# Feed-forward stages: the second half of an item's row maxima is transposed into the mixed bank instead of the tokens bank

## The reference

```python
x = _layernorm(x + self_attention(x))               # stage 1, causal
x = _layernorm(x + cross_attention(x, ctx, mask))   # stage 2, 64 keys
for l in range(2):                                  # inside _L0_ffn_ref
    x = x + _attn(_ln(x, ln1_w[l], ln1_b[l]), ...)  # stages 3 and 4, causal
    h = _ln(x, ln2_w[l], ln2_b[l])
    x = x + (_token_moe if l == 0 else _seq_moe)(h, ...)
x = _layernorm(...)
```

## Time and profile before

| | |
|---|---|
| median of 3 runs | 1364.99 us (1358.8, 1364.99, 1370.07) |
| profiled execution, device time | 1360.42 us |
| its span, first to last instruction | 1358.6 us |
| mean granted TensorE clock | 0.948 |
| PE busy | 1226.1 us (90%), 9884 instructions |
| DVE busy | 931.0 us (69%) |
| ACT busy | 806.2 us (59%) |
| POOL busy | 685.0 us (50%) |
| chain that ended last, by engine | PE 63%, DVE 14%, POOL 10%, issue 6%, ACT 4% |
| `L638` PE into tokens, count | 384, 54.1 us busy, 21.4 us idle before |
| `L830` ACT copy of a half | 577 ns each |

### The profile page before, as it was taken

One profiled execution on the slowest core, in us unless ns is written; L12 is line 12 of the kernel. 1 busy time (PEld: TensorE's weight loads), 2 busy tenths in 40 slices (PEclk: granted clock), 3 DMA queues, 4 the chain that ended last, 5 costly groups with the idle time before them and its releaser, 6 DMA issues.

```text
span 1358.6 us, 30590 instructions
## 1 busy us (share of the span) xinstructions
PE 1226.1 (90%) x9884; PEld 996.7 (73%) x9884; DVE 931.0 (69%) x2791; ACT 806.2 (59%) x1629; POOL 685.0 (50%) x1233
## 2 busy tenths in 40 slices
PE   2999999998888789999999899979999999989997
PEld 1777777776666467777777799878777777768886
DVE  5789998987667778888995221123888888645553
ACT  3577776664565356666666565544666666664443
POOL 4355555563222136777778310220567666445554
PEclk9899999986787779999998999998999999999999
DMA  4687777524555444545541787777565555346764
GB/s 110 177 226 236 215 229 201 130 69 128 151 159 145 123 118 126 133 132 135 132 125 46 200 239 226 230 223 210 155 147 148 145 147 150 101 117 187 203 195 118
DMA packets 212707, 216.94 MB, mean 160 GB/s; under 512 B 46403, under 2 KB 163395, under 8 KB 212548
## 3 DMA queue, kind: packets, MB, share of 16 engines
q1 hardware_dynamic: 197712, 199.52, 54.4%
q0 software_dynamic: 4096, 8.40, 2.2%
q10 hardware_dynamic: 10740, 7.06, 1.7%
HBM read 126.90 MB, written 85.46 MB: 156 GB/s over the span
## 4 chain that ended last, share of the span: by engine, by line
PE 63%; DVE 14%; POOL 10%; issue 6%; ACT 4%; SPq 1%; DMA 1%; ACTq 1%; DVEq 0%; POOLq 0%
PE weights L1556 6%; PE scores L609 5%; PE weights L663 4%; PE values L699 4%; PE scores L1799 3%; PE weights L1815 3%; PE weights L668 3%; POOL out_room L1251 3%; POOL probs L1160 3%; PE values L706 3%; PE scores L618 3%; PE scores L1540 3%; DVE negmax L1004 3%; PE tokens L562 2%; PE mixed L718 2%
## 5 line engine op out<-in xcount | busy, mean ns | idle before, releaser
L1160 POOL TENSOR_SCALAR_AFFINE_SELECT probs<-probs 128x256 f32<-128x256 f32 (+1 forms) x576 | 279.0, 490 | 233.8 <-ACT probs L849 230.2
L849 ACT ACTIVATE probs<-weights 128x512 f32<-128x512 f32 x448 | 264.6, 597 | 118.0 <-PE weights L663 84.3
L1004 DVE TENSOR_REDUCE negmax<-scores 128x4 f32<-128x512 f32 x384 | 260.8, 684 | 78.1 <-PE scores L609 74.7
L609 PE MATMUL scores<-keys,queries 128*128 128x512 f32 (+1 forms) x384 | 185.1, 485 | 3.5 <-DVE negmax L1004 1.0
L849 ACT ACTIVATE probs<-weights,keybias 128x512 f32<-128x512 f32 x192 | 131.3, 688 | 65.5 <-PE weights L663 48.4
L663 PE MATMUL weights<-queries,keys 104*128 104x256 f32 x768 | 159.1, 290 | 0.9 <-issue 0.6
L663 PEld LDWEIGHTS weights<-queries,keys 104*128 104x128 f32 x768 | 139.9, 194 | 22.3 <-issue 3.6
L1008 DVE TENSOR_REDUCE negmax<-scores 128x2 f32<-128x512 f32 (+1 forms) x192 | 130.7, 684 | 29.9 <-PE scores L615 20.2
L668 PEld LDWEIGHTS weights<-queries,keys 104*128 104x128 f32 x768 | 114.4, 195 | 10.3 <-ACT probs L849 0.4
L668 PE MATMUL weights<-queries,keys 104*128 104x128 f32 x768 | 109.9, 267 | 0.3 <-ACT probs L849 0.3
L699 PE MATMUL values<-probs,v 128*32 128x256 f32 x1536 | 105.4, 393 | 2.3 <-POOL probs L1160 2.3
(11 more groups left out here) (275 smaller groups left out, 2791.2 us busy)
## 6 DMA issues: line engine op xcount, KB each, us to landing
windows<-parts SPq DMA_DIRECT2D x192, 192.0 KB
queries<-windows SPq DMA_DIRECT2D x64, 384.0 KB
hidden_room<-in_m_w SPq DMA_DIRECT2D x78, 256.0 KB, 2.9
out_room<-in_m_w SPq DMA_DIRECT2D x78, 256.0 KB, 3.1
keys<-windows SPq DMA_DIRECT2D x192, 96.0 KB
routed_rows<-zeros SPq DMA_DIRECT2D x64, 256.0 KB, 3.6
windows<-parts SPq DMA_DIRECT2D x64, 120.0 KB
expert_rows<-probs ACTq DMA_DIRECT2D x46, 128.0 KB, 3.4
```

The source lines that it names most:

```text
L609: i = pe.matmul(bank[:], queries[0:rows, s, t * P:(t + 1) * P], keys[0:rows, s::S4, half * P:(half + 1) * P], start=True, stop=True)
L849: act.activation(probs[:, n % RING], weight_banks[n % 2][:], ACT.Exp, scale=SCALE, **bias).then_inc(exp_done.sem, 1)
L1004: i = dve.tensor_reduce(most[:, part, s, :], bank[:].rearrange("p (a k) -> p a k", k=P), AX.X, ALU.max, negate=True)
L1160: pool.affine_select(out=block, in_=block, compare_op=ALU.is_ge, fill=0.0, base=0, pattern=[[0, heads], [1, P]], channel_multiplier=-1).th ...
```

## The change

The bank is now a function of the item and of the half. For ffn items the first half stays in `tokens` and the second goes to `mixed`; self and ctx items are as before. The matmuls and copies are the same in number and shape, and no slot or rank changes. What moves are the waits of `take` and `until`: the second half asks for `mixed`, and the next user of `mixed` asks for the second half's copy.

```diff
-        def maxima_bank(g):
-            return mixed_bank if units[g].kind == "ctx" else tokens_bank
+        def maxima_bank(g, half):
+
+            return mixed_bank if units[g].kind == "ctx" or units[g].kind == "ffn" and half else tokens_bank
 
         def pe_maxima(pe, g):
 
-            bank = maxima_bank(g)
-            X = bank.tensor
             pe.wait_ge(maxparts_ready.sem, maxparts_ready.at(g))
             for half in range(2):
+                bank = maxima_bank(g, half)
+                X = bank.tensor
                 bank.take(pe)
...
         def act_maxima(act, g):
-            X = maxima_bank(g).tensor
             act.wait_ge(stacked.sem(g), stacked.at(g))
             for half in range(2):
+                X = maxima_bank(g, half).tensor
                 act.wait_ge(maxT_ready.sem, maxT_ready.at(g, half + 1))
```

## The result

The changed kernel takes **1404.41 us** in the median (1397.72 to 1415.99, four runs) against 1367.17 us of the kernel before, measured beside it. The ratio is 1.0292, 95% interval 1.0206 to 1.0377: slower by 37 us, where 1367.7 us was forecast. The profiled execution has a span of 1396.0 us (before 1358.6), and its mean granted clock is 0.926 (before 0.948). Lines of the changed kernel are numbered one higher from L625 on: L639 is the product of the maxima, L831 the copy, L752 the logits.

The account below looks back on a forecast made before the run. PE carries 63% of the chain, though in many items another engine sets the pace. Losses of 6.43 us less gains of 1.35, 0.43 and 1.96 gave +2.7 us, 1367.7 us as median; range 1357 to 1377 us.

Parts of the forecast that it names:

- The order of events: Routed items: second half starts 0.43 us earlier, second copy stays behind ACT's exponential, logits start 0.83 us later.
- The step that failed: PE's clock in routed items: no falls counted in the sum, up to two (3.2 us) kept in the range.
- The prediction's own sign of being wrong: The forecast is wrong if, among other signs, the clock in 526 to 740 us falls below 0.97.
- The rival with the clock: Clock falls in routed items at slot 14, 1.6 us each; seven falls give 1378.9 us; chance 0.07.
- the forecast's own +2.7: Net sum for the whole kernel: losses 6.43 us less gains of 1.35, 0.43 and 1.96 us.
- The wait itself: Logits wait for the second copy in 13 routed items: 6 x 0.64, 3 x 0.83 and 0.1 us, together 6.43.
- The slack that I gave DVE: Routed items: DVE absorbs 0.19 of 0.83 us in six; in four the chain goes elsewhere, 0.1 us together.
- the rival that counts it in full: Routed items: 13 x 0.83 = 10.8 us lost and no gains, 1375.8 us; chance 0.11.
- Layer 1: Gain vanishes at L545 in twelve items; the last four, without gathers, gain 3 x 0.43 + 0.67 = 1.96 us.
- The 0.43: Earlier start of the second half, at L663's end (544.49) instead of 544.91, 0.43 us a time.
- The first items: Layer 0's first three ffn items: the first gains 1.35 us, the second 0.43, the third nothing.
- The rule that was weighed and set aside: Skill's rule on short idle stretches between matmul groups; by it the routed items would lose more than the wait itself.

Follow-up runs that it names:

- the filled pause: The change plus 12 products of constants by PE into the tokens bank, in the wait ahead of the router's logits: 1373.84 us, ratio 1.0085.
- change in 19 items only: The change kept only in the ffn items without a route step (g = 32 to 34, 48 to 63), others as before: 1360.29 us, ratio 0.9968.
- control with later logits: The kernel before with the router's logits one slot later (15 instead of 14) and nothing else: 1367.08 us, ratio 1.0007.
- the wait alone: The kernel before with its banks, plus a wait of the logits for the second half's copy in the 13 routed items: 1407.91 us, ratio 1.028.
- The pause in layer 1: The change in the unrouted items only, plus a PE wait for the second copy behind the second half in layer 1's 16 items: 1383.74 us, ratio 1.0209.
- the last experiment: The change, with ACT's copies of the maxima ahead of the exponential of their slot in layer 0: 1389.8 us, ratio 1.02.
- later logits: The change with the router's logits written one slot later (15 instead of 14): 1366.32 us, ratio 1.0014.
- logits behind the values too: The change with the logits one slot later and the next item's values' projection ahead of them in slot 15: 1363.93 us, ratio 0.9968.
- four only: The change with 4 products of constants in the wait ahead of the logits instead of 12: 1386.58 us, ratio 1.0135.

## Why the prediction was wrong

**The order of events was right.** The second half no longer waits; `mixed` is free in time; the second copy stays where ACT's exponential puts it; L752 gets a wait in exactly 13 items. Forecast were about 1.3 us each, some 16 us; measured 20.9 us.

**The step that failed** is the one on the clock: "I count none in the sum, since layer 1 has pauses of 0.43 and about 0.7 us in twelve items at a clock of 1.00". So the fall of the clock, a term of the sum, stood at nothing on the ground of pauses elsewhere. The pause of the change is 1.6 us ahead of the logits, and with it the clock fell in 11 of 12 distances, for 25.6 of the 36.8 us. The prediction's own sign of being wrong, a clock below 0.97 in these items, came true with 0.85. The rival with the clock had the right place and mechanism, and chance 0.07. Two readings would have raised it, as is easily said afterwards. In the earlier trace rows two almost equal stretches, PE busy 2.73 and 2.76 of 4 us, went different ways: a fall was already close in these items, so an edit that adds idling to each of them had to be priced as a fall in many, not in none. And the fall was priced at 1.6 us from one 4 us window at 0.60, with seven falls needed for 1%; in the change one fall is mostly low over about 7 us, and the 12 distances cost 25.6 / 12 = 2.1 us each. All 13 at that price and the forecast's own +2.7 would have given +30 us.

**The wait itself** was mis-sized: 6.4 us forecast, 11.2 us measured with the filled pause, 0.93 a distance. The slack that I gave DVE (0.19 us in six items, full cover in four) was not there: with 12 products 11 of the 12 distances grew, also those in which the chain before went through a scatter or through DVE, and the twelfth is the one that had the fall before (19.4 us; 18.0 us without a fall, 18.6 us here). A slack read from one chain holds for that chain; the next one was hardly shorter. In size the wait came out at the price of the rival that counts it in full, 10.8 us.

Each wait was also longer than forecast. The logits start 1.87 us behind the first half before and, by the forecast, 0.83 us later; they came 1.1 us later (2.97 us). Of the difference about 0.2 us is that ACT reached the first copy later. It starts 0.82 us after the start of the first half's products in the profiled execution of before, and 0.94 to 1.05 us in all but the first and the last routed items of nine of the other eleven executions, also in three with the banks of before in those items (change in 19 items only, control with later logits, the wait alone). The pause in layer 1 has 0.82 us again, and in the last experiment the edit moves the copy. What sets this I can't say; it isn't the bank. The rest is the time from the second copy's end to the logits, 0.14 us instead of the 0.05 us read between the halves.

**Layer 1** was right in its mechanism: gains disappear at L545. Its wait there is 1.40 us an item in the changed kernel, where 0.69 to 0.73 was usual before; the stretch shortened by 2.25 us in the change and by 2.7 to 3.0 in three others with it (19 items only, later logits, logits behind the values too), for 1.96 forecast from the last four items. Only 3 x 0.43 = 1.29 of that lie in this stretch, since the last item's 0.67 comes behind its end, so the gain was mis-sized too: the last three distances became 0.8 to 0.9 us shorter each. A part is the reading: the second half starts 0.58 us earlier (0.87 instead of 1.45 us behind the first), not 0.43. The 0.43 was counted from the listed end of L663, but the next products start 0.25 us behind the start of a round (558.80, then 559.05) while the round is listed with 0.41.

**The first items** gained more than forecast: the three distances from g = 32 to g = 35 sum to 2.9 us less, where I had 1.35 + 0.43 = 1.78. The distances were 19.1, 15.8 and 15.8 us and became 17.1, 14.9 and 15.8; the third gave nothing, as forecast. A part of the first is the clock: before, that distance ran at 0.64 in the mean (475.73 to 494.85 us), in the changed kernel at 0.80, which the forecast of 1.35 us did not separate. Together that is 5.1 us for 3.7 forecast; by the ratio of the kernel with the 19 items alone it is about 4.

**The rule that was weighed and set aside.** "TensorE: Matmul & The Clock Gate" of the Trainium skill, in its section on psum-queue depth-cycling, says that short idle stretches between groups of matmuls can send the clock back and forth, and that the loss lies there. I weighed it against the trace and let the trace of before win, because it showed the fall in one place of 13. The runs here side with the rule on idle stretches: 0.85 with the pause, 1.00 with the wait filled. The cycling through banks is not what did it here, since the wait alone, with the banks of before, gave 0.85 too.

## What to carry to other kernels

Before moving a buffer to another bank, list who asks for that bank next, and look up in the other engine's order when the last reader is done. Making the producer earlier doesn't make an in-order reader earlier, and the wait only changes its owner.

Count what a wait costs or gives back from start to start of the neighbouring products, not from the listed end of one.

On a PE-bound kernel, price an added pause of TensorE as the pause plus a fall of the clock, above all where the trace already shows one fall. If PE's busy time rises with the same number of instructions, look at the clock first. A filled pause is the test that separates the two.

## What the runs showed of the hardware

The clocks are of the one profiled execution of each kernel. Pauses of 1.6 us in one piece, or of 0.62 and 0.71 us with 0.6 us of products between, in items of 17 us, went with a mean granted clock of the stretch of 0.85 instead of 0.99. Pauses of 0.9 us gave 0.94, and 1.3 us in layer 1 gave 0.94 instead of 1.00; but 1.17 us ahead of the logits, with the copies moved, went with 0.81, and 1.40 us at L545 with 1.00. So the length of a pause alone does not tell whether the clock falls. Twelve products of constants in the pause kept it at 1.00, four only at 0.89. Products that nobody reads, put into a wait, brought back about 28 of the 40 us that the ratio of the change stands for.
